# A three-layer decoder block on one core: squares and neighbour products of the second batch in another order

## What is computed

```
x = layernorm(x + attention(x))            # 32 heads of 32, 8 key heads, rotary angles, causal softmax
x = layernorm(x + conv(x * similarity(ctx)))  # 3 taps; similarity of neighbouring context columns
x = layernorm(x + ffn(x))                  # 8 gated low-rank experts

# similarity: for each batch, over the 128 rows of the context
norm[s] = sqrt(sum_c ctx[c, s]^2);  sim[s] = sum_c ctx[c, s] * ctx[c, s+1] / (norm[s] * norm[s+1])
```

## Time and profile before

| | before |
|---|---|
| median of 3 runs | 1435.54 us (1435.25 to 1436.57) |
| the profiled execution | 1439.9 us |
| its span in the profile | 1438.1 us |
| busy share: PE, DVE, ACT, POOL | 95%, 76%, 65%, 69% |
| mean granted clock of TensorE | 0.978 of full |

### The profile page before, as it was taken

One profiled execution on the slowest core, in us unless ns is written; L12 is line 12 of the kernel. 1 busy time (PEld: TensorE's weight loads), 2 busy tenths in 40 slices (PEclk: granted clock), 3 DMA queues, 4 the chain that ended last, 5 costly groups with the idle time before them and its releaser, 6 DMA issues. The chain is left out here.

```text
span 1438.1 us, 32297 instructions
## 1 busy us (share of the span) xinstructions
PE 1370.1 (95%) x8288; PEld 1061.4 (74%) x8288; DVE 1092.5 (76%) x3869; ACT 932.5 (65%) x3258; POOL 985.9 (69%) x936
## 2 busy tenths in 40 slices
PE   6899999999999999999985899999999999999995
PEld 4677777777777777777753688888888888888874
DVE  5677777777777777777766477878887788887784
ACT  5678878788787887878765354555554455555542
POOL 3677767777677776777754566777766777776753
PEclk9999999999999999999996899999999999999997
DMA  6345445454454544545465857656666766666751
GB/s 227 113 121 156 122 139 152 119 155 122 141 152 119 152 125 141 151 119 153 125 179 164 218 145 170 165 153 163 159 159 165 175 150 159 165 156 162 157 117 44
DMA packets 108861, 213.03 MB, mean 148 GB/s; under 512 B 26640, under 2 KB 32272, under 8 KB 108816
## 3 DMA queue, kind: packets, MB, share of 16 engines
q1 hardware_dynamic: 108816, 212.51, 54.0%
HBM read 131.83 MB, written 34.47 MB: 116 GB/s over the span
## 5 line engine op out<-in xcount | busy, mean ns | idle before, releaser
L432 PE MATMUL wo_ps<-weights,halves 128*128 128x512 f32 x2304 | 573.8, 400 | 11.9 <-DVE weights L611 11.8
L432 PEld LDWEIGHTS wo_ps<-weights,halves 128*128 128x128 f32 x2304 | 423.8, 189 | 129.3 <-issue 34.3
L694 ACT ACTIVATE pexp<-sm,smin 128x128 f32<-128x128 f32 x1024 | 398.7, 393 | 119.1 <-DVE smin L562 118.4
L1039 PE MATMUL wo_ps<-weights,halves 128*128 128x512 f32 x1488 | 401.1, 402 | 2.0 <-DVE yz L1142 2.0
L811 POOL TENSOR_TENSOR pn<-pexp,prec 128x512 f32<-128x512 f32 x256 | 267.8, 1046 | 151.6 <-DVE prec L569 151.5
L1392 POOL TENSOR_TENSOR prods<-prod,prods 128x512 fp32r<-128x512 f32 x192 | 259.9, 1362 | 134.0 <-ACT prods L1286 129.1
L1039 PEld LDWEIGHTS wo_ps<-weights,halves 128*128 128x128 f32 x1488 | 273.4, 190 | 61.2 <-issue 3.7
L562 DVE CUSTOM_DVE_ANT_0 sm<-s_ps,mask_t 128x128 f32<-128x128 f32 x1024 | 231.8, 281 | 80.0 <-PE s_ps L462 80.0
L1286 ACT CAST prods<-prod 128x512 fp32r<-128x512 f32 x192 | 118.8, 621 | 165.9 <-DVE prod L1176 129.4
L1176 DVE TENSOR_TENSOR prod<-att,x 128x512 f32<-128x512 f32 x192 | 186.2, 985 | 14.0 <-DMA att<-sim_scratch 11.1
L694 ACT ACTIVATION_READ_ACCUMULATOR pexp<-sm,smin 128x1 f32 x1024 | 194.8, 190 | 0.0
(11 more groups left out here) (99 smaller groups left out, 1668.6 us busy)
## 6 DMA issues: line engine op xcount, KB each, us to landing
att<-sim_scratch SPq DMA_DIRECT2D x192, 252.0 KB
pt<-blocks SPq DMA_DIRECT2D x640, 64.0 KB, 2.0
ctx_t<-in_ctx SPq DMA_DIRECT2D x32, 576.0 KB, 4.5
raw<-in_xT SPq DMA_DIRECT2D x32, 512.0 KB, 3.7
raw<-ot_scratch SPq DMA_DIRECT2D x32, 512.0 KB, 6.6
xn<-in_x SPq DMA_DIRECT2D x32, 512.0 KB, 7.2
out<-late SPq DMA_DIRECT2D x32, 512.0 KB, 6.2
ot_scratch<-ot SPq DMA_DIRECT2D x63, 256.0 KB, 2.1
```

Source lines behind the costliest of these rows:

```text
L432: mm = pe.matmul(qkv_ps[(par + g) % 2][:], xs[:, par, xl, k], w_sb[:, wl, g, k], start=(k == 0 and n == 0), stop=(k == KT - 1 and n == 2))
L694: ins = nc.scalar.activation(pexp[:, c % 2, i * P:(i + 1) * P], sm[:, c % 2, i * P:(i + 1) * P], ACT.Exp, bias=smin[:, c % 2, i:i + 1], sc ...
L1039: mm = pe.matmul(wo_ps[n][:], os_t[:, par, ol, k], wo_sb[:, wl, k, n * BANK:(n + 1) * BANK], start=(k == 0 and m == 0), stop=(k == KT - 1 ...
```

## The change

It concerns step 0 and step 1 of part 1 alone.

- ScalarE: `square(1)` moves from the head of step 1 to behind `exponent(0, 2)`, ahead of `copy_q(0, 1)`.
- GpSimd: the two `neighbour(0)` move from the end of step 0 to step 1, behind `add_q(0, 1)`. The two `neighbour(1)` move from chunk 1 to chunk 4, behind `scale(0, 3)`.
- VectorE: `sum_neighbours(0)` moves from chunk 0 of step 1 to chunk 1, behind `invert(0, 0)`; `sum_neighbours(1)` from chunk 3 to chunk 6, behind `invert(0, 5)`.

```diff
@@ VectorE, step @@
-                if at_step(t, 1) and p == 0:
+                if at_step(t, 1) and p == 1:
                     sum_neighbours(0)
-                if p == 3 and valid(t):
+                if p == 3 and valid(t) and not at_step(t, 1) or at_step(t, 1) and p == 6:
                     sum_neighbours(t)
@@ ScalarE, step @@
-            if valid(t):
+            if valid(t) and not at_step(t, 1):
                 square(t)
...
                 if valid(a):
                     exponent(a, p)
+                if at_step(t, 1) and p == 2:
+                    square(1)
@@ GpSimd, step @@
                 add_k(0, 0)
                 add_q(0, 0, 0)
-                neighbour(0, 0)
-                neighbour(0, 1)
                 return
...
                 if p == 0 and valid(a):
                     add_q(a, 1 - par, 1)
+                if at_step(t, 1) and p == 0:
+                    neighbour(0, 0)
+                    neighbour(0, 1)
...
-                if at_step(t, 1) and p == 1:
+                if at_step(t, 1) and p == 4:
                     neighbour(1, 0)
                     neighbour(1, 1)
```

## The result

| | before | changed |
|---|---|---|
| median of 22 runs each | 1435.59 us (1432.65 to 1437.92) | 1439.39 us (1437.23 to 1443.26) |
| ratio, 95% interval | | 1.003 [1.0023, 1.0037] |
| the profiled execution | 1439.9 us | 1440.26 us |
| its span | 1438.1 us | 1438.4 us |
| mean granted clock | 0.978 | 0.979 |

The account below looks back on a forecast made before the run. TensorE's losses in steps 1 and 2 were taken as never made up. A longer gap in step 1, 1.68 us, plus waits in step 2, 2.07, sum to 3.75: 1435.54 becomes 1439.3 us, range 1436.8 to 1441.4.

Parts of the forecast that it names:

- Bound: Part 1: what TensorE loses or wins in step 1 or 2 is never made up in the loop.
- First place: TensorE's gap at 44.88 before score(0, 1): x of batch 2 issued 1.89 us later, gap grows by 1.68 us.
- the step named: Step 1, VectorE: reduction of batch 0 behind the reciprocal awaiting first exponents, at 41.01 instead of 39.12.
- The 3.5 us of the row for the load: Step 1: x of batch 2 lands 3.5 us after issue; the skill's 3.2 would make the gap grow by 1.4.
- Second place: SyncE's queue into step 2: late sums of batch 1 delay ten transfers and x of batch 3; TensorE idles 2.07 us.
- The split: Step 2, two new idle times on TensorE: 0.6 us before L475 and about 1.5 before L462.
- The forecast for the profiled span: Whole kernel: the profiled span of 1438.1 us becomes 1441.9, by adding 3.75.
- One step: Step 2, GpSimd: neighbour(2, 0) waits for its context, scale(0, 5) 1.4 to 2.3 us late, covered by ScalarE's wait for x.
- Clock: Behind the first gap: low stretch of 4.3 us keeps its cost at the later restart, 0.8 us either way.
- the rival of two drops: Step 2: TensorE's 2.07 us of waiting lowers the clock again, 1.6 us more, 1440.9; chance 0.14.
- Only the first place: SyncE catches up within 1.35 us of slack, so step 2 costs nothing: +1.4 to +2.1, 1437.2; chance 0.22.
- Faster: Step 1: squares use idle time if x lands before 45.2; 1432.2 alone, 1434.3 with step 2's loss; chance 0.12.

Follow-up runs that it names:

- e4: Changed kernel with the reduction of batch 0 back in chunk 0 of step 1; median +1.1 us, ratio 1.0013 to the kernel before.
- e2: Kernel before with only the products of batch 1 moved to chunk 4 and its reduction to chunk 6; median +0.6 us, ratio 1.0011.
- e7: Changed kernel with the load of x of batch 3 ahead of the sums of batch 1 in SyncE's queue; ratio 1.0014 to the kernel before.
- e6: Changed kernel, x of batch 2 loaded early, batch 1's products and reduction back, squares behind query copy and fourth exponents; ratio 0.9964 to the kernel before.
- e10: Changed kernel once more, unchanged, for a second profile and times; median +3.6 us, ratio 1.0023 to the kernel before.
- e1: Changed kernel with the products and reduction of batch 1 back in chunks 1 and 3; median +1.1 us, ratio 1.0011 to the kernel before.
- e3: Changed kernel with the load of x of batch 2 issued right behind the first context; median -1.4 us, ratio 0.9991 to the kernel before.
- e8: Kernel e6 with the copy of the values of batch 0 issued ahead of the sums of batch 0; ratio 0.9953 to the kernel before.

## Why the prediction was right

**Bound.** That nothing lost in steps 1 and 2 is made up in the loop holds: from the first scores of step 3 to the end of the stretch all eleven profiles with a change take 607.59 us, so every shift made before step 3 is kept.

**First place.** With the 0.47 us by which this execution was early, the forecast rows fall on the measured ones: exponents at 39.24, measured 38.78 + 0.47; x issued at 43.38, measured 42.91 + 0.47; resumption at 52.34, measured 51.85 + 0.47. The gap grew by 1.65, forecast 1.68. The reduction starts at 40.56, forecast 41.01 less 0.47. e4 shows that the step named, the reduction behind the first exponents, is the cause. The 3.5 us of the row for the load was the better price: from issue at 42.91 to ScalarE's start at 46.40 are 3.49. The estimate of 3.2 from the Trainium skill (DMA: Bandwidth & Descriptors, Anatomy of one DMA), which the page makes for another issuer, was too short here.

**Second place.** Forecast 2.07, measured 2.44 and 1.81 in the two profiles of the kernel, with the ten transfers issued in 7.35 and 6.82 us where 6.97 were taken. The split was right in kind (0.6 and 1.5, against 0.90 and 1.38, then 0.48 and 1.33), e2 shows it alone and e7 takes the second of the two waits away. The rows themselves came later than forecast: the reduction of batch 1 at 62.53 on the forecast's time (61.71 forecast), x of batch 3 issued at 72.25 (71.10), ScalarE's high half at 75.97 (74.6). The low clock had lasted 1.0 longer, which moves TensorE and the queue behind it alike, and the ten issues and the load took 0.6 longer.

**The size.** 3.75 forecast against 3.80 measured is closer than the working deserves. The interval of the ratio allows 3.3 to 5.3 us, and the loops of the two profiles of the changed kernel are 4.8 and 2.9 longer than that of the kernel before; they differ by the clock behind the gap and by the waits of step 2. The mechanism and the rough size were right; that the medians meet the sum within 0.1 is luck. The forecast for the profiled span, 1441.9, was 3.5 too high: it took the kernel before's long end over into another execution.

**One step was wrong in its cause.** I had `neighbour(2, 0)` wait for its late context. GpSimd's timeline after says otherwise:

```profile
63.42 1.30 POOL L794 TENSOR_TENSOR nb<-ctx_t 128x512 f32<-128x512 f32 x1 [1.64 <-DVE csum L590]
```

It waits for the reduction of batch 1, which frees the products' buffer, and that ended at 63.27, later than the context's landing (issued at 58.88, landed 3.8 later, 62.7). The lateness forecast was about right, 1.64 for 1.4 to 2.3, and its cover too: ScalarE waits for x behind it. In e7, where x is early, TensorE has no wait at the second scores either, though its wait of 1.32 just before gives ScalarE more time there.

**Clock.** I took the same cost for the later restart, with 0.8 either way. The first profile shows 1.0 more (5.08 for 12 matmuls instead of 4.05), the second 0.2 less (3.84). The clock did not fall a second time in step 2: the granted clock is 1.00 from 66 to 84 us. So the rival of two drops did not come. What the Trainium skill says of waits (TensorE: Matmul & The Clock Gate, HAM oscillation — how this bites in real kernels), in an example with waits of some 3 to 5 us, agrees with the gaps of 2.90 and more in step 1, which all had the lower clock behind them. No fall followed the waits of 0.90 and 1.38 in step 2, nor the 1.89 in step 1 of e6. The price that the rival took from rows 11 is not a steady one. In the second profile of the changed kernel (e10) TensorE waits as long at the same place near the end of part 1:

```profile
732.31 1.17 PE L462 MATMUL s_ps<-kt,qt 32*128 32x128 f32 x32 [2.28 <-ACT qt L681]
733.41 3.06 PE L432 MATMUL wo_ps<-weights,halves 128*128 128x512 f32 x12
```

The granted clock stays at 1.00 there, and the 12 matmuls take 3.06; in the kernel before, behind 2.26, it fell to 0.50 from 731 to 734 us, and they took 4.62. What decides between the two is not shown.

**Rivals.** "Only the first place" is e1, another kernel than this one. "Faster" was tied to the landing of x before 45.2; ScalarE could use it at 46.40 in this execution, 46.87 on the time of the kernel before. e3 brings it in early, and then the rival's own working holds: 2.9 less than the 5.79 of before was worked out for the gap, and 2.90 is what was left.

## What to carry to other kernels

A move that lets one engine start sooner gains nothing while a later link waits for a transfer: follow the transfer back through its issuing queue to whatever that queue waits for, as here a reduction on VectorE that the same change had made later. A single in-order queue of transfers ties unrelated chains, so a sum that nobody needs soon delays the load behind it that somebody does; the load with no condition left can go ahead of the one with a condition. And where the effect is 0.3% of the time, compare a stretch that holds the change and ends where the loop is steady; two spans can hide it altogether.

## What the runs showed that was not expected

- After the same kind of gap the lower clock lasts differently from execution to execution: the first 12 full matmuls behind the first 32 scores took 3.69 to 5.11 us in ten profiles, 3.84 and 5.08 in two of the same kernel. The gap was 2.90 in the kernels with 5.11 and with 3.69, so its length alone doesn't tell the cost.
- The steps' beginning shifts too: the first scores of step 1 start between 35.29 and 39.26 us in the eleven other profiles beside 36.88, with nearly the same code ahead of them. The two late ones, 39.26 in e2 and 38.26 in e8, had a low clock ahead of them behind a wait of 1.98, where the changed kernel and e1 waited 1.99 and 1.97 and kept the clock. This, the clock behind the gap and the end of part 1 may together make the spread of the kernel before, 5.3 to 8.7 us in four sets of runs; it was profiled once, so that is not shown.
